# A transformer block with routed experts on one core: units of 256 and 128 rows, the first of them under the last routing, the shared network behind them

## What is computed

```python
h = _layernorm(x, axis=-1) * (1 + cb) + sb
x = x + gb * _L0_ffn_ref(h, ...)
# in _L0_ffn_ref, with 8 experts, I = 256, the 2 likeliest experts of a token:
shared = silu(x @ shared_gate.T) * (x @ shared_up.T) @ shared_down.T
probs = sigmoid(x @ router_w.T + routing_bias)
scores, indices = top_k(probs, 2);  scores = scores / sum(scores)
g = silu(einsum('th,ehi->tei', xf, gate_w));  u = einsum('th,ehi->tei', xf, up_w)
combined = einsum('tei,eih,te->th', g * u, down_w, w)
return shared + combined
```

## Time and profile before

| | us |
|---|---|
| median of 3 runs | 681.9 (681.18 to 684.36) |
| profiled execution, span from first to last instruction | 683.7 |
| span's share: attention, up to the first shared product | 483.4 |
| shared network and last routing, up to the first unit's products | 49.1 (to 532.55) |
| units | 124 (to about 657.5) |
| tail | 26 |
| busy in the span: PE, DVE, ACT, POOL | 624.5, 516.7, 411.0, 264.0 |

### The profile page before, as it was taken

The page is one execution under the profiler, slowest core; times in us unless marked ns, Lnnn a source line. Parts: engine busy times, 40 slices in busy tenths (PEclk is TensorE's granted clock), DMA queues, the critical chain, the costliest instruction groups (busy, mean ns, idle before and its releaser), DMA issues.

```text
span 683.7 us, 11593 instructions
## 1 busy us (share of the span) xinstructions
PE 624.5 (91%) x3693; PEld 298.9 (44%) x3693; DVE 516.7 (76%) x1104; ACT 411.0 (60%) x846; POOL 264.0 (39%) x309
## 2 busy tenths in 40 slices
PE   4988999999999999999999999999998898888935
PEld 2332333233333333433333333232465888888931
DVE  5659888889988989888898888983368655555617
ACT  2145777777777687777777777778542445444520
POOL 4221022324352461452434233134434366566540
PEclk9669999999999999999999999999999999999987
DMA  3533132222321233223222231115102222222228
GB/s 101 146 56 97 52 101 76 66 82 72 94 86 62 75 97 95 79 78 105 72 70 75 70 98 52 39 40 173 53 0 70 64 74 78 69 78 79 70 68 320
DMA packets 50064, 56.92 MB, mean 83 GB/s; under 512 B 10281, under 2 KB 39243, under 8 KB 50004
## 3 DMA queue, kind: packets, MB, share of 16 engines
q1 hardware_dynamic: 42648, 43.11, 22.4%
q0 software_dynamic: 4320, 8.47, 3.6%
q10 hardware_dynamic: 3036, 4.61, 2.1%
HBM read 38.36 MB, written 17.92 MB: 82 GB/s over the span
## 4 chain that ended last, share of the span: by engine, by line
PE 68%; DVE 13%; ACT 6%; DMA 4%; issue 4%; SPq 2%; POOL 1%; another core or an unknown queue 0%; ACTq 0%; POOLq 0%; DVEq 0%
PE pv L1457 15%; PE st L1446 14%; PE mx L1431 13%; PE st L1646 9%; DVE neg_max L1012 6%; PE mx L1590 3%; ACT pt L803 2%; PE misc L1324 2%; PE misc L1351 2%; PE pv L1655 2%; PE misc L1655 2%; PE st L1600 1%; PE misc L1357 1%; DMA even_qk<-k_parts 1%; DVE ln L969 1%
## 5 line engine op out<-in xcount | busy, mean ns | idle before, releaser
L803 ACT ACTIVATE pt<-st 128x512 f32<-128x512 f32 x496 | 282.2, 598 | 106.0 <-PE st L1446 96.8
L1012 DVE TENSOR_REDUCE neg_max<-mx 128x2 f32<-128x1024 f32 x248 | 294.4, 1215 | 50.5 <-PE mx L1431 47.3
L1457 PE MATMUL pv<-pt,vs 128*32 128x512 f32 x1024 | 136.4, 605 | 0.3 <-ACT pt L803 0.3
L690 POOL DMA_INDIRECT routed<-rec,row_u x64 | 64.4, 1007 | 142.1 <-PE pv L1457 115.2
L750 POOL DMA_INDIRECT results<-qs,home_u x71 | 77.4, 1091 | 60.5 <-ACT qs L932 42.1
L1446 PE MATMUL st<-even_qk 74*128 74x512 bf16 x256 | 88.9, 388 | 4.1 <-DMA even_qk<-m_rows 2.2
L1446 PE MATMUL st<-qs,ks 74*128 74x512 bf16 x240 | 81.5, 383 | 1.8 <-ACT pt L803 1.1
L1431 PE MATMUL mx<-even_qk 72*128 72x512 bf16 x240 | 74.5, 392 | 6.0 <-DVE neg_max L1012 3.4
L1431 PE MATMUL mx<-ks,qs 72*128 72x512 bf16 x256 | 76.5, 380 | 2.8 <-DVE neg_max L1012 2.5
L1258 DVE TENSOR_TENSOR vs<-vs,st 128x256 f32<-128x256 f32 x71 | 29.7, 418 | 42.6 <-ACT vs L927 31.4
L1646 PE MATMUL st<-vs,pt 128*128 128x128 f32 x376 | 52.0, 282 | 10.3 <-DVE vs L1258 7.4
(11 more groups left out here) (199 smaller groups left out, 792.7 us busy)
## 6 DMA issues: line engine op xcount, KB each, us to landing
ks<-routed SPq DMA_DIRECT2D x71, 65.0 KB
even_qk<-q_parts SPq DMA_DIRECT2D x48, 96.0 KB
qs<-q_parts SPq DMA_DIRECT2D x48, 96.0 KB
ks<-k_parts SPq DMA_DIRECT2D x48, 96.0 KB
even_qk<-k_parts SPq DMA_DIRECT2D x42, 96.0 KB
q_parts<-qk_parts SPq DMA_DIRECT2D x21, 128.0 KB
k_parts<-qk_parts SPq DMA_DIRECT2D x7, 384.0 KB, 2.3
x_in<-L_attn_x SPq DMA_DIRECT2D x8, 256.0 KB
```

The source lines that it names most:

```text
L690: pool.indirect_dma_start(out=routed_dram, out_offset=bass.IndirectOffsetOnAxis(ap=row_u[:, k, t:t + 1], axis=0), in_=rec[b.par][:, k, t, ...
L803: act.activation(pt[n % 2][:, hh, :], score_bank(b, n, hh), ACT.Exp, scale=SCALE).then_inc(exp_done, 1)
L1012: dve.tensor_reduce(neg_max[g % 2][:, hh, 2 * half:2 * half + 2], mx_bank[half][:], AX_X, ALU.max, negate=True).then_inc(mx_free, 1)
L1457: last = pe.matmul(pv_bank[32 * hh:32 * (hh + 1), :], vs[b.par][:, j, HG * g + hh, :], pt[n % 2][:, hh, :], start=(n % Y_SLOTS == 0), stop ...
```

## The change

- *Units.* 28 units of 256 rows (two blocks of 128) and 15 of 128 rows: `UNITS` = 43, of which 16 `EARLY_PAIRS` and 12 `LATE_PAIRS` come first. A pair has one load, two transposes, up products of 256 columns, one silu and one product of 512 columns, one weight copy, eight down records, two scalings and two sends. Transposes of all units share one bank (`xT_bank`), so `unit_T` waits for `xuT_ready` of the unit before. The ring still has 8 slots, `ARING` is 3 instead of 4.
- *Early pairs.* Their tables (`early_tables`, four parts) come from `next_row` behind batch 5 and are computed in slots 8, 9, 10 and 12 of the last batch's attention. They take whole blocks of 256 rows that are already scattered. The rest, late pairs and singles, is planned by `late_tables` (five parts) in DVE's unit steps 7 to 11, when batch 7 has its rows.
- *Order.* Shared batches 0 to 2 stay ahead of the units. `layer_norm2` of batch 7 stands on DVE behind the first two weight copies and `shared_sum(1)`. Its `h2_T` is in PE's unit step 1, the logits in step 2, the ranks in step 6; on DVE the choice is in steps 2 to 4 and `assign_rows` in step 6. POOL scatters batch 7 ahead of the send of unit 4. SP writes the paddings ahead of loads 13 and 14 and waits for them and the last scatters ahead of load 16.
- *Shared batches 3 to 7* stand behind the units, with three pairs of banks in turn; their down product is no longer gated and added on its own.
- *Tail.* SP loads all 16 results. POOL adds the two results of every batch. DVE, for batches 0 to 2 (`finish_first`): gate, add, store; for 3 to 7 (`finish`): add the shared down product, gate, add. `OUT_ORDER` is (3, 0, 4, 1, 5, 2, 6, 7), and the products of shared batches 5, 6 and 7 stand on DVE between the finishes.

The core of the diff:

```diff
-UNITS = K_TOP * TOKENS // P + E
-MOST_UNITS = K_TOP * TOKENS // P + E - 1
-ARING = 4
+ARING = 3
+PAIR = 2 * P
+EARLY_PAIRS, LATE_PAIRS = 16, 12
+PAIRS = EARLY_PAIRS + LATE_PAIRS
+UNITS = PAIRS + K_TOP * TOKENS // P + E - 1 - 2 * PAIRS
+FIRST_SHARED = 3
...
-        OUT_ORDER = (0, 2, 1, 4, 3, 6, 5, 7)
+        OUT_ORDER = (3, 0, 4, 1, 5, 2, 6, 7)
...
@@ SP
+            sp.wait_ge(early_ready, 1)
+            sp.wait_ge(rows_free, 2 + B - 2)
+            sp.wait_ge(st_full, HG * SLOTS * B)
+            for u in range(UNITS):
+                if u == 13:
+                    pad_regions(range(0, E // 2))
+                if u == 14:
+                    pad_regions(range(E // 2, E))
+                if u == EARLY_PAIRS:
+                    sp.wait_ge(padding_written, 16 * (E + 1))
+                    sp.wait_ge(scattered, BATCH_ROWS * B)
+                    sp.wait_ge(tables_ready, 2)
+                if u == PAIRS:
+                    sp.wait_ge(tables_ready, 3)
+                load_unit(u)
...
@@ POOL
             rstd(mv2, ve2, var2_ready, rstd2, rstd2_ready, stats2_ready, B_LAST)
+            rows_scattered(B_LAST.plus(-1))
             modulate2(B_LAST)
-            scatter(B_LAST)
...
+            for u in range(UNITS):
+                if u == 4:
+                    scatter(B_LAST)
+                send_unit(u)
+
+            for b in OUT_ORDER:
+                pool.wait_ge(results_loaded[b], 16 * K_TOP)
+                pool.tensor_tensor(results[b][0], results[b][0], results[b][1], ALU.add).then_inc(sums_ready, 1)
...
@@ DVE
+            for i in range(UNITS):
+                ahead = i + 2
+                if ahead < UNITS:
+                    if ahead == EARLY_PAIRS:
+                        dve.wait_ge(tables_ready, 4)
...
+                    unit_weights(ahead, experts)
+                unit_act(i)
+                if ahead < UNITS:
+                    unit_rows(ahead)
...
+                if i == 6:
+                    assign_rows(B_LAST, use(B_LAST, "rank_last"))
+                if i in (7, 8, 9, 10, 11):
+                    late_tables(i - 7)
...
+            def finish(b):
+
                 r = results[b][0]
...
+                add_results(b)
+                dve.wait_ge(s_down, b + 1)
+                dve.tensor_tensor(r, down_bank(b)[:].rearrange("p (t c) -> p t c", t=TT), r, ALU.add).then_inc(s_gated, 1)
+                dve.wait_ge(s_gated, b + 1)
+                gate_and_add(b)
+
+            for j in range(IC):
+                shared_act(3, j)
+            for j in range(IC):
+                shared_act(4, j)
+            finish(3)
+            for j in range(IC):
+                shared_act(5, j)
+            finish_first(0)
+            finish(4)
+            for j in range(IC):
+                shared_act(6, j)
+            finish_first(1)
+            finish(5)
+            for j in range(IC):
+                shared_act(7, j)
+            finish_first(2)
+            finish(6)
+            finish(7)
...
@@ PE
+            def unit_T(u):
+
+                slot = u % RING
+                pe.wait_ge(xu_loaded[slot], 16 * (u // RING + 1))
+                if u >= 1:
+                    pe.wait_ge(xuT_ready, u)
+                for h in range(halves(u)):
+                    last = pe.transpose(xT_bank(u)[:, h * P:(h + 1) * P], xu[slot][:, h, 0:C], ident[:])
+                last.then_inc(xuT_full, 1)
```

More of the change, by code:

```diff
@@ L590, in _ @@
             sp.dma_start(routed_dram[E * REGION:E * REGION + P, :], pad_row[:]).then_inc(padding_written, 16)
[L591 to L596, removed]
@@ new lines, in unit_y @@
+            def unit_y(u):
+                act.wait_ge(yu_full, u + 1)
+                for h in range(halves(u)):
+                    last = act.activation(y_u[u % RING][:, h, :], y_bank(u)[:, h, :], ACT.Copy, scale=xu[u % RING][:, h, C:C + 1])
+                last.then_inc(yu_ready, 1)
+            for u in range(2):
+                unit_xT(u)
+            for i in range(UNITS + 2):
+                if i < UNITS:
+                    unit_silu(i)
+                if i + 2 < UNITS:
+                    unit_xT(i + 2)
+                if i == UNITS + 1:
+                    shared_silu(FIRST_SHARED, 0)
+                if i >= 2:
+                    unit_y(i - 2)
+                if i == 1:
+                    evacuate_h2T(B_LAST, use(B_LAST, "h2T_last"))
+                if i == 3:
+                    exp_minus_logits(B_LAST, use(B_LAST, "lg_last"))
@@ new lines, in starts, with take @@
+            def starts():
+                step(dve.tensor_tensor(entered[:, 0:E, :], earlier[:], padded[:].unsqueeze(1).to_broadcast([P, E, E]), ALU.mult))
+                step(dve.tensor_reduce(region_end[:], entered[:, 0:E, :], AX_X, ALU.add))
+            def take(rows, into):
+                step(dve.tensor_scalar(into[:], region_end[:], -1.0, float(rows), ALU.mult, ALU.add))
+                step(dve.tensor_scalar(into[:], into[:], 0.0, None, ALU.max))
+                step(dve.tensor_tensor(into[:], into[:], padded[:], ALU.min))
@@ new lines, in early_tables @@
+            def early_tables(part):
+                if part == 0:
+                    dve.wait_ge(misc_free, use(B_LAST.plus(-1), "rank") + 1)
+                    step(dve.tensor_tensor(padded[:], next_row[B % 2][:], first_row[:], ALU.subtract))
+                    whole_blocks(padded[:], padded[:], PAIR, 0.0)
+                if part == 1:
+                    starts()
+                    take(EARLY_PAIRS * PAIR, taken[0])
+                if part == 2:
+                    skips(None)
+                    places(0, EARLY_PAIRS, 2)
+                if part == 3:
+                    rows_from(0, EARLY_PAIRS, 0.0, early_ready)
+                    unit_experts(0, EARLY_PAIRS, early_ready)
```

499 lines of the change are left out of this document (244 added, 255 removed).

## The result

The changed kernel takes 675.9 us (median of 20 runs, 673.42 to 684.87) beside 682.65 us for the kernel before (20 runs): a ratio of 0.9893, 95% interval 0.9874 to 0.9912. So it is 1.1% faster, where 5% were forecast, and its time lies above the range. The profiled execution has a span of 676.1 us, 7.6 less than before, and a mean granted clock of 0.958 instead of 0.971.

What follows compares the result with a forecast made beforehand. PE and, nearly as close, POOL's sends bound the units; five shared batches and the tail were needlessly serial. PE's units to 618.9, shared network 26.1, ending 2.1 + 2.4 gave 649.5, less 1.8: 647.7 us, range 640 to 661.

Steps and rivals of the forecast that it cites:

- The units come forward: Start of the unit stage on PE: unit 0 begins at 502.0, ahead of the last batch's scatters.
- A pair costs 2.83 us: PE's unit steps: up products 1.72, two transposes 0.22, down 0.89; 28 pairs and 15 singles make 100.9 us.
- Ranks and rows: Last batch's routing: ranks at 521.6 on PE, cast rows at 523.0, or 524.0 with early pauses.
- The halts cost 9.2 us: ACT's pauses in the unit stage: 9 x 0.4 us in pairs and 4 x 1.4 in singles, instead of 21.4.
- My second case: Rival: ACT's pauses cost the full 21.4 us as before; span 660.7, median 658.9; chance 0.22.
- The case of 677 us: Rival: a wait holds unit 0 until the last rows are scattered, start 534 instead of 502, +32 us; chance 0.03.
- One PE wait near step 12 to 14: Unit 12 waits until unit 4's send has landed and frees its slot; priced at 3.4 us of PE (0 to 7).
- The clock: Rival: gaps waiting for POOL's sends put PE at 1.2 GHz for its remaining units, +64 us, 712; chance 0.03.
- Sends end at 619.5: POOL's chain: 63 sends at 1.35 us each after the last batch's scatters end at 534.4.
- The tail: After the last send: first result at 624.3, first sum 625.8, 27 DVE operations of 0.70 to 644.7, last store 2.4 more.
- The exclusion: Rival: POOL's eight sums and DVE's two-input operations block each other, up to 12 us, total 657; chance 0.06.
- The sum without halts: Predicted span of the whole kernel: 647.1 us by POOL's path, 649.5 by PE's; the later one counts.

Runs made afterwards that it cites:

- e5: The changed kernel, unchanged, on a chip without halts: 649.8 us, beside 664.4 for the kernel before, a ratio of 0.981.
- e16: The changed kernel, unchanged, on a third chip with halts: 677.75 us, 0.9855 of the kernel before.
- e13: The changed kernel, unchanged, once more on a chip with halts: 676.3 us, 0.989 of the kernel before.
- e9: The changed kernel with 4 late pairs and 31 single units instead of 12 and 15, on a chip with halts: 679.7 us, 0.984 of the kernel before.
- e14: The changed kernel with the last batch's scatters split, four before unit 6's send and four before unit 8's: 674.9 us, beside 676.3 unsplit.
- e15: The changed kernel with POOL waiting behind every second last-batch scatter until the two have landed: 678.5 us, beside 676.3 without these waits.
- e8: The changed kernel without POOL's eight sums of the two results, on a chip without halts: 646.8 us, beside 649.8 with them.
- e1: The kernel before without its 71 sends of results, on a chip without halts: 659.9 us, beside 665.65 with them.
- e18: The kernel before without its sends of results, on a chip with halts: 661.6 us, beside 687.5 with them.
- e10: The changed kernel without its 71 sends, the last batch's 8 scatters kept, on a chip with halts: 646.7 us, beside 688.6 for the kernel before.
- e11: The changed kernel with each send a plain DMA of POOL instead of an indirect one, on a chip with halts: 651.4 us, beside 683.7 for the kernel before.

## Why the prediction was wrong, point by point

- **The units come forward: right.** Unit 0's products begin at 504.75 (forecast 502.0). e5 has them at 501.65. Of the 3.1 us between the two, 2.5 lie in attention, whose end varies from one execution to the next (first shared product from 482.4 in e16 to 488.5 in e13), and only 0.6 are halts under the scatters of batch 6.
- **A pair costs 2.83 us: right** where nothing halts (PE's transposes at 529.56 and 532.40 are 2.84 apart). What the size of units is worth was not measured; e9 can't tell it.
- **Ranks and rows: right in e5** (place at 522.11, row_u at 522.96, for 521.6 and 523.0), late by 5 us in the first trace (527.61, 528.35), 2.5 of them from attention, the rest halts.
- **The halts cost 9.2 us: this step failed.** I took the 21.4 us that the stage before lost and shrank them by the smaller number of instructions and the slack. They are what chips of one kind add to both kernels: the spans of the kernel before with and without them differ by 683.7 - 662.5 = 21.2 us, those of the changed kernel by 676.1 - 647.5 = 28.6, of which 2.5 are attention; the medians differ by 682.65 - 664.4 = 18.3 and 675.9 - 649.8 = 26.1. So nothing of them went away, and some 5 to 8 us came on top. Slack was of little use, because the longest halts last as long as POOL's row, 11 us, and not the 2 us that I had worked out for one. The likely reason for what came on top is the row of 14: the scatters now stand among the sends, POOL falls behind, and it was near its limit before as after (1.28 of 1.445 us per block, 2.54 of 2.84 per pair). That is argued, not shown: neither e14 nor e15 took the long row away. My second case, the full 21.4 us, was the right one in kind, and at 658.9 us still 17 too low. The case of 677 us, in which the units don't come forward, lies nearest to the measured time by chance: they did come forward. The prediction named the warning itself: it said that it could not say what halts ACT, and then gave it a price.
- **One PE wait near step 12 to 14, 3.4 us (0 to 7): right in place, wrong in kind and size.** It is 13.37 us, and it is not the wait for POOL's sends or SP's load but ACT under the row of 14. In e5 two waits of 1.10 and 1.49 us stand there, the second of them the ring's wait that I priced, and some 2.6 us more at the lower clock, which I had not counted.
- **The clock: I said that no gap would be left.** The 13.37 us gap brought the lower level (0.81 from 545 to 580, down records at 1.92 for 1.06 us). It is the gap's consequence and is in the 28.6. In e5 the gaps of 1.10 and 1.49 us do the same for some 5 us.
- **Sends end at 619.5.** In e5 they end at 616.8 (1.27 to 1.28 each, my 1.35 was high); in the first trace at 645.4.
- **The tail.** In e5 DVE's first result is at 622.78 (forecast 625.8), its 27 operations take 22.2 us to 645.0 (forecast 18.9 to 644.7). The exclusion that I had as a rival at 657 is real, but worth 3.0 us (e8), not 12: only five of DVE's operations meet a sum, and they take 4.3 us more. I had also taken 1.48 us for a sum from the earlier trace rows, the mean of 1.23 and of an addition that had itself waited; undisturbed sums take 1.26. The longer tail is made good by the sends' earlier end.
- **The sum without halts: right, in part by luck.** It gives a span of 649.5 us, 647.1 by POOL's path; e5's is 647.5. Sends that end 2.7 us early and a tail that lasts 3.3 us longer than forecast cancel each other. The median of e5 is 649.8, beside 647.7: I took 1.8 us off the span, but an execution's time is some 2 us longer than its span (649.43 for 647.5). What was wrong is which chip the number was for, and that the gain of 34 us held 19 us of halts (21.4 less the 2.4 by which the forecast lay above POOL's chain) that I thought would go: the structure gives 662.5 - 647.5 = 15.0, the halts take back 28.6 - 21.2 = 7.4 (2.5 of it attention), and 7.6 is left. By the medians it is 14.6 less 7.8, which leaves the measured 6.75.

## What to carry to other kernels

An idle time on an engine whose operand is long ready is a cost with a cause outside the order of the kernel; before pricing it, list what the other engines do in the same time, here rows of POOL's indirect DMAs. Compare it with the end of what it waits for first: the profile's "issue" stood here beside halts and beside ordinary waits. Work that is put in front of an engine which is already near its limit makes a backlog, and this can pay back what the change wins elsewhere. And compare a kernel with its reference on more than one chip before reading a few per cent as the kernel's.

## What the runs showed of the hardware that was not expected

- Two kinds of chips: on three of the five of e1 to e18, and on that of the first traces, ACT stands still for most of a long row of POOL's indirect DMAs, and SP's DMA issues are slower beside it (7.96 us for four instead of 3.68); on two it does not, even for 53 in a row. The same program differs by 18 us (before) and 26 us (changed) in its median. What makes a chip so, and by what path POOL holds up ACT, is open.
- In a halt neither the 0.30 us between DMAs nor a memset of 0.12 us frees ACT, though a single instruction passes now and then; a pause of 1.56 us let one scaling through; with waits of POOL of 1.8 to 2.7 us behind every second DMA ACT was not halted (e15).
- A row of 8 cost ACT 5.8 us in e10 and 5.7 in e11, and nothing in the kernel before; the row of 14 cost 11.0, and the two sends behind it 4.4 more.
- A plain DMA issued by POOL takes 0.54 us of it, an indirect one 0.97 and 0.30 behind it, and no long halt was seen under plain ones, whose rows were short.
